# V projection of a cross attention as a 2x2 block product with seven block products, sums of blocks on POOL

## The reference

```python
x = x + _L0_xattn_ref(_layernorm(x), ctx_4096, Wq, Wk, Wv, Wo)
# in it, with H, KV, HD = 16, 4, 96 and G = H // KV
hidden = jnp.concatenate([context, latents], axis=1)      # (64, 289, 512)
q = (latents @ Wq.T).reshape(b, q_len, H, HD)
k = (hidden @ Wk.T).reshape(b, s_len, KV, HD)
v = (hidden @ Wv.T).reshape(b, s_len, KV, HD)             # (64, 289, 384)
# softmax(q k^T / sqrt(96)) v per head, then @ Wo.T
```

## Time and profile before

| | |
|---|---|
| three timed runs | 2138.29, 2140.99, 2141.76 us (median 2140.99) |
| the profiled execution | 2136.47 us, its span 2134.4 us |
| PE busy, over the span | 2059.4 us (96%) |
| DVE, ACT, POOL busy | 1308.7 us (61%), 683.7 us (32%), 248.3 us (12%) |
| mean granted TensorE clock | 0.989 |

### The profile page before, as it was taken

How to read it: one execution, slowest core, us unless ns; L and a number is a source line. 1 busy time by engine, 2 the same in 40 slices (tenths; PEclk the granted TensorE clock), 3 DMA queues, 4 the chain that set the end, 5 groups by cost and what they waited for, 6 DMA issues and landing times. The chain is left out here.

```text
span 2134.4 us, 33623 instructions
## 1 busy us (share of the span) xinstructions
PE 2059.4 (96%) x10660; PEld 1480.4 (69%) x10660; DVE 1308.7 (61%) x4451; ACT 683.7 (32%) x1861; POOL 248.3 (12%) x360
## 2 busy tenths in 40 slices
PE   7999999999999999999999999999899999779998
PEld 5778677777767778677777867777566666466665
DVE  3736547484654747456483755747577777677885
ACT  2333333333332433333242433333223223122222
POOL 0000000000000000000000000000233333133332
PEclk9999999999999999999999999999999999889999
DMA  7101000010000101001010000120100000000000
GB/s 289 31 15 31 23 24 30 24 30 24 24 20 24 30 24 30 24 24 30 14 37 16 30 23 24 30 86 1 45 1 1 1 0 29 0 1 21 21 15 25
DMA packets 51991, 62.14 MB, mean 29 GB/s; under 512 B 14193, under 2 KB 47665, under 8 KB 51042
## 3 DMA queue, kind: packets, MB, share of 16 engines
q1 hardware_dynamic: 51938, 61.46, 9.1%
HBM read 54.00 MB, written 4.29 MB: 27 GB/s over the span
## 5 line engine op out<-in xcount | busy, mean ns | idle before, releaser
L345 PE MATMUL psLane<-hid,WkT 128*128 128x289 f32 x1536 | 404.0, 408 | 0.0
L352 PE MATMUL psLane<-WvT,hid 128*128 128x384 f32 x1024 | 348.7, 486 | 0.0
L345 PEld LDWEIGHTS psLane<-hid,WkT 128*128 128x128 f32 x1536 | 284.1, 190 | 72.7
L352 PEld LDWEIGHTS psLane<-WvT,hid 128*128 128x128 f32 x1024 | 189.8, 190 | 109.7
L537 ACT ACTIVATE probs<-psLane,nmax 128x289 f32<-128x289 f32 x256 | 126.2, 498 | 423.6 <-DVE nmax L640 423.6
L505 ACT ACTIVATE KT<-psLane 96x289 f32<-96x289 f32 (+2 forms) x384 | 155.8, 406 | 153.3 <-PE psLane L345 151.0
L298 POOL TENSOR_TENSOR tails<-probs,unit 128x66 f32<-128x66 f32 x128 | 38.1, 297 | 1387.3 <-ACT probs L537 1387.3
L678 DVE MAX8 top<-work 128x8 f32<-128x257 f32 x512 | 180.3, 414 | 2.7
L335 PE MATMUL psLane<-xnT,WqT 128*128 128x128 f32 x1536 | 176.6, 275 | 0.0
L335 PEld LDWEIGHTS psLane<-xnT,WqT 128*128 128x128 f32 x1536 | 174.8, 192 | 0.3
L663 DVE TENSOR_TENSOR X<-X,psLane 128x512 f32 (+1 forms) x16 | 11.0, 689 | 261.6 <-PE psLane L417 261.6
(11 more groups left out here) (190 smaller groups left out, 3138.2 us busy)
## 6 DMA issues: line engine op xcount, KB each, us to landing
hid<-in_ctxT SPq DMA_DIRECT2D x64, 514.0 KB, 3.8
y<-X SPq DMA_DIRECT2D x16, 256.0 KB, 2.0
X<-in_x SPq DMA_DIRECT2D x1, 3840.0 KB, 14.9
WqT<-in_WqT SPq DMA_DIRECT2D x4, 768.0 KB, 11.4
WoT<-in_WoT SPq DMA_DIRECT2D x1, 3072.0 KB, 21.7
Vtail<-Vlat SPq DMA_DIRECT2D x128, 24.0 KB
w_qkv<-in_w_qkv SPq DMA_DIRECT2D x2, 1536.0 KB, 6.5
w_ffn<-in_w_ffn SPq DMA_DIRECT2D x2, 1024.0 KB, 8.0
```

Of the source, the lines that this page charges most:

```text
L345: mm = pe.matmul(out[:, 0:S], WkT[:, c, P * k:P * k + P], hid[:, j, c, :], start=(c == 0), stop=(c == DC - 1))
L352: mm = pe.matmul(out[:, 0:KW], hid[:, j, c, P * s:P * s + P], WvT[:, c, :], start=(c == 0), stop=(c == DC - 1))
```

## The change

The V projection of rows 0 to 255 of a batch, (256 x 512) by (512 x 384), is taken as a product of 2x2 blocks: rows by their half `s`, features by their half `k`, columns by their half `n` (VH = 192). Instead of eight block products there are seven (Winograd's form of Strassen's scheme), each of 2 matmuls of 128x192. Four sums of blocks of `hid` per batch (`vsums`) and, once, four sums of weight blocks (`vweights`) are made on POOL. The seven products go through PSUM in four fills (`V_FILLS`), ACT copies each fill into `vproducts`, and POOL adds them up into `V` in seven steps. `vweights`, `vproducts` and `vsums` lie in the space of `early["w_ffn"]` and `early["w_o"]`, weights of the next phase, so their loads are issued later (`square_in`), after the last batch's V.

```diff
+VH = KW // 2
+V_FILLS = ((1, 6), (7, 5), (3, 4), (2,))
...
+            def sum_rows(t, j):
+
+                b = TB * t + j
+                rows = lambda s, k: hid[:, j, 2 * k:2 * k + 2, P * s:P * s + P]
+                pool.wait_ge(ctx_in[j], 16 * (t + 1))
+                before = (t, 7 * j - 1) if j else (t - 1, 27)
+                if not (isinstance(t, int) and (t, j) == (0, 0)):
+                    pool.wait_ge(kv_filled, kv(*before) + 1)
+                pool.tensor_tensor(vsums[0], rows(1, 0), rows(1, 1), ALU.add).then_inc(vsum_step, 1)
+                pool.tensor_tensor(vsums[2], rows(0, 0), rows(1, 0), ALU.subtract).then_inc(vsum_step, 1)
+                pool.wait_ge(vsum_step, 4 * b + 2)
+                pool.tensor_tensor(vsums[1], vsums[0], rows(0, 0), ALU.subtract).then_inc(vsum_step, 1)
+                pool.wait_ge(vsum_step, 4 * b + 3)
+                pool.tensor_tensor(vsums[3], rows(0, 1), vsums[1], ALU.subtract).then_inc(vsum_step, 1)
...
+            def add_first(t, j):
+
+                b = TB * t + j
+                pool.wait_ge(kv_evac, kv(t, 7 * j + 3) + 1)
+                pool.tensor_tensor(u2, product(1), product(6), ALU.add).then_inc(vpost_step, 1)
+                pool.wait_ge(kv_evac, kv(t, 7 * j + 4) + 1)
+                pool.wait_ge(vpost_step, 3 * b + 1)
+                pool.tensor_tensor(u3, u2, product(7), ALU.add).then_inc(vpost_step, 1)
+                pool.wait_ge(vpost_step, 3 * b + 2)
+                pool.tensor_tensor(u4, u2, product(5), ALU.add).then_inc(vpost_step, 1)
+                wait(pool, av_done, 4 * b - 4)
+                pool.tensor_tensor(v_block(j, 1, 1), u3, product(5), ALU.add).then_inc(v_ready, 1)
+
+            def add_second(t, j):
+
+                b = TB * t + j
+                pool.wait_ge(kv_evac, kv(t, 7 * j + 5) + 1)
+                pool.wait_ge(vpost_step, 3 * b + 3)
+                pool.tensor_tensor(v_block(j, 0, 1), u4, product(3), ALU.add).then_inc(v_ready, 1)
+                pool.tensor_tensor(v_block(j, 1, 0), u3, product(4), ALU.subtract).then_inc(v_ready, 1)
+                pool.wait_ge(kv_evac, kv(t, 7 * j + 6) + 1)
+                pool.tensor_tensor(v_block(j, 0, 0), product(1), product(2), ALU.add).then_inc(v_ready, 1)
...
-            def v_part(t, j, s):
-                out = next_bank(t, 5 * j + 3 + s)
-                for c in range(DC):
-                    mm = pe.matmul(out[:, 0:KW], hid[:, j, c, P * s:P * s + P], WvT[:, c, :],
-                                   start=(c == 0), stop=(c == DC - 1))
...
+            def v_part(t, j, f):
+                out = next_bank(t, 7 * j + 3 + f)
+                for i, n in enumerate(V_FILLS[f]):
+                    if n == 6:
+                        pe.wait_ge(vsum_step, 4 * (TB * t + j) + 4)
+                        if isinstance(t, int) and (t, j) == (0, 0):
+                            pe.wait_ge(vweight_step, 4)
+                    mm = v_product(out[:, VH * i:VH * i + VH], j, n)
                 mm.then_inc(kv_filled, 1)
...
                 if g == 0:
-                    pe.wait_ge(kv_evac, kv(t, 5 * j + 4) + 1)
+                    pe.wait_ge(v_ready, 4 * b + 4)
...
-            def evac_v(t, j, s):
+            def evac_v(t, j, f):
+                act.wait_ge(kv_filled, kv(t, 7 * j + 3 + f) + 1)
+                if f == 0:
+                    wait(act, v_ready, 4 * (TB * t + j))
+                n = len(V_FILLS[f])
+                act.activation(vproducts[:, 2 * f:2 * f + n, :].rearrange("p a n -> p (a n)"),
+                               psKV[:, kv_bank(t, 7 * j + 3 + f), 0:VH * n], ACT.Copy).then_inc(kv_evac, 1)
...
+                    sp.wait_ge(kv_filled, kv(NT - 1, 27) + 1)
+                    sp.wait_ge(v_ready, 4 * B)
+                    for k, name in (("w_o", "w_o0"), ("w_ffn", "w_ffn0")):
+                        sp.dma_start(early[k][:], a[name]).then_inc(square_in, 16)
```

More of the change, by code:

```diff
@@ L112, in phase_a @@
         V = sb("V", [P, 2, 2, KW])
+        spare = [early[k][:].rearrange("p c n -> p (c n)") for k in ("w_ffn", "w_o")]
+        vweights = spare[0][:, 0:8 * VH].rearrange("p (i c n) -> p i c n", i=4, c=2)
+        vproducts = spare[1][:, 0:7 * VH].rearrange("p (i n) -> p i n", i=7)
+        vsums = [spare[i // 2][:, (8 - i // 2) * VH + 2 * P * (i % 2):][:, 0:2 * P].rearrange("p (c n) -> p c n", c=2)
+                 for i in range(4)]
         Vlat = sb("Vlat", [P, KW])
@@ L300, in body @@
             def body(t, first, last):
+                add_first(t, 0)
+                add_second(t, 0)
                 for j in range(TB):
[L302 to L305, removed]
+                    gather_tails(t, j, 0)
+                    if j < TB - 1:
+                        sum_rows(t, j + 1)
+                    else:
+                        add_second(t, j)
+                        if not last:
+                            sum_rows(t + 1, 0)
+                    if j == 1:
+                        next_rstd() if last else rstd_of(t + 1)
+                    gather_tails(t, j, 1)
+                    if j < TB - 1:
+                        add_first(t, j + 1)
+                    if j < TB - 2:
+                        add_second(t, j + 1)
@@ L347, in k_part, with v_product @@
                 mm.then_inc(kv_filled, 1)
[L349 to L353 removed]
+            def v_product(out, j, n):
+                rows = lambda s, k: lambda c: hid[:, j, 2 * k + c, P * s:P * s + P]
+                summed = lambda i: lambda c: vsums[i][:, c, :]
+                block = lambda k, n: lambda c: WvT[:, 2 * k + c, VH * n:VH * n + VH]
+                combined = lambda i: lambda c: vweights[:, i, c, :]
+                left, right = {1: (rows(0, 0), block(0, 0)), 2: (rows(0, 1), block(1, 0)), 3: (summed(3), block(1, 1)),
+                               4: (rows(1, 1), combined(3)), 5: (summed(0), combined(0)), 6: (summed(1), combined(1)),
+                               7: (summed(2), combined(2))}[n]
+                for c in range(2):
+                    mm = pe.matmul(out, left(c), right(c), start=(c == 0), stop=(c == 1))
+                return mm
+            def v_part(t, j, f):
[6 more added lines that the diff above has]
+                    mm = v_product(out[:, VH * i:VH * i + VH], j, n)
                 mm.then_inc(kv_filled, 1)
@@ L436, in body @@
                 k_part(t, 0, 2)
-                v_part(t, 0, 0)
-                v_part(t, 0, 1)
+                for f in range(4):
+                    v_part(t, 0, f)
                 if first:
@@ L555, in body @@
                     evac_k(t, 0, k)
-                evac_v(t, 0, 0)
-                evac_v(t, 0, 1)
+                for f in range(4):
+                    evac_v(t, 0, f)
                 if first:
@@ L584, in body @@
                         evac_v(t, j + 1, 0)
+                        evac_v(t, j + 1, 1)
                     else:
```

96 lines of the change are left out of this document (61 added, 35 removed).

## The result

The changed kernel takes 2099.07 us (median of 4 runs, 2098.84 to 2099.63); the kernel before, in the same set, 2139.64 us (4 runs, 2133.64 to 2141.76). The ratio is 0.982, with a 95% interval of 0.980 to 0.984. The forecast was 2110, the range 2103 to 2124: the direction was right, the gain larger than the range allowed. The medians differ by 40.6 us; profile against profile it is 2136.47 - 2099.63 = 36.8 us, where the prediction's sum had 29.5. Later sets put the median of the kernel before at 2135.23 to 2137.89, so 2 to 4 of the 40.6 us are the spread of its runs.

The account below looks back on a forecast made before the run. PE was taken as the bound, busy 92.19 of a tile's 92.30 us. A tile saves 3 x 0.55 + 0.27 = 1.92 us, 16 tiles 30.7, net 29.5; forecast 2110 us, range 2103 to 2124 for 8 in 10.

Parts of the forecast that it names:

- the pace of V: V's matmuls on PE: 165 ns per 192-column record, 28 records in 4.62 us instead of 5.17, 0.55 us saved per batch.
- the last batch of a tile: values starts 0.27 us sooner, held by POOL's adds; less 0.05, plus 0.05 at v_latents, 0.27 us gained per tile.
- start and end: First batch's wait for Vtail and lower clock behind it, 1 us charged; last tile's exponentials holding PE, 0.3 us less gained.
- sums hidden: POOL's 11 operations per batch, 6.8 us of some 16 us, delay nothing in batches 0 to 2 of a tile.
- The baseline: Profiled 2136.5 less 29.5 gives 2107; the timed median, 4.5 us higher, gives 2111.5; 2110 was taken.
- The lower bound of the pace: V's 192-column records on PE at cycles alone, 160 ns each: 0.69 us saved per batch, 44 us in all.
- The full gain: Rival: with adds of 0.5 us and a sooner OT copy the last batch saves 0.55 too; 35 us, 2105 us, 10%.
- no wait at product 6 or for a bank: PE finds POOL's sums ready at product 6, and ACT's copies free the two PSUM banks in time, 0.3 us to spare.
- The estimate that the prediction drew from the Trainium skill: V's matmuls at 87 ns for 192 columns against 114 for 384: slower by 0.6 us per batch; not used in the sum.
- DVE and POOL hold each other up: Rival: a hold of one add at mask, 0.57 us, loses 9 us, two such places 18; 2119 to 2128, 18%.
- The slower rival: POOL's three adds become the path at values of a tile's last batch; with three holds 22 us lost, 2163, 6%.

Follow-up runs that it names:

- Experiment 1: The kernel before with each V fill made as two halves of 192 columns, all eight block products, no sums: 2140.08 us, 1.0012.
- experiment 4: The first tile's Vtail loads issued ahead of those of X and WoT: in the changed kernel 2095.46 us, in the kernel before 2132.44 us.
- Experiment 2: The changed kernel without any of POOL's sums, PE's work the same, V not computed: 2099.77 us, 0.983.
- experiment 3: The changed kernel with more POOL adds ahead of the last three of every batch: one add 2108.63 us, four adds 2181.37 us.
- experiment 7: The changed kernel with one more DVE operation of 192 elements behind mask per batch: two SBUF inputs 2101.29 us, one input 2100.08 us.
- experiments 5 and 6: Changed kernel with values released before POOL's last add, 2106.29 us; changed kernel with DVE's OT copy ahead of MAX8 in a tile's last batch, 2108.18 us.

## Why the forecast was too cautious

Of the 10.9 us between 2110 and 2099.1, 7.3 us are in the sum and 3 in what it was set against; the rest is rounding and the spread of runs. The 7.3 are three terms: 2.9 for the pace of V, 3.2 for the last batch of a tile, 1.2 for start and end. The mechanism was right (PE is the bound, sums hidden, the last batch gains less); two of its terms were mis-sized, and none of them alone would have left the range.

- **The pace, mis-sized.** "On the line between the two it costs [...] 165 ns": measured 162.5. The line was drawn through the 128-column stream, which pays 5 ns over its cycles, while 192 columns pay 2.5 like 384. A batch saves 0.61 us, not 0.55, which for the 48 batches that the sum gave this term is 2.9 us. Experiment 1 found the same pace with no change to anything else.
- **The last batch, read at the wrong instruction.** The two starts were right within 0.12 us, but the gain was read off `values`, 0.27 us, with 0.05 given and 0.05 taken. The next in the queue, `v_latents`, starts when DVE's `hid` copy ends, before as after, and it is its start that the next tile inherits. That copy follows `xt` and not `values`. The prediction had 0.37 us for `xt`; carried on to `v_latents` by the 2.04 us between the two in the earlier trace rows it gives S+6.37 against S+6.74, 0.37 and not 0.27. Measured is 0.49 at both: the other 0.12 is `xt` itself, since the `OT` copy started at S+3.62 and took 0.54 us, where the prediction had S+3.7 and 0.56. Less 0.02 for the first half of V that is 0.47, 0.2 us more for each of 16 tiles, 3.2 us. With both terms a tile is 3 x 0.61 + 0.47 = 2.30 us instead of 1.92.
- **The start and the end, 1.2 us charged and none lost in sum.** The prediction charged 1 us for the start and 0.3 at the end (30.7 less these is 29.4, not 29.5). The waiting that it named is there: the first `values` starts 0.30 us sooner (50.35 against 50.65), where it is 0.78 without the wait (47.32 against 48.10, experiment 4). But the stretches at the two ends gain 3.21 + 1.84 = 5.05 us where nothing waits, 0.45 more than two tiles, and that makes up for it; the 0.3 at the end did not come, since 1.84 is three times 0.61. The prediction also took the clock as the same in both kernels. It fell behind the start's wait in the kernel before alone, and behind the last projection's wait in the changed one alone; that these two cancel is luck.
- **The baseline.** The sum gave 2107 from the profiled execution; I went up to 2110 for the median of the timed runs, 2141. Later sets of the kernel before have medians of 2136.11 (15 runs), 2135.23 (9) and 2137.89 (17): the profiled time of 2136.5 was near the middle, and three runs were few to move a forecast on. 3 us.
- **The range.** The lower bound of the pace, 160 ns, gave 44 us of gain in the prediction's own words, and the measured pace lies halfway to it; a range that ended at 2103 left that out. "The full gain" (2105) was one of the rivals, given 10%; it gave the last batch its whole 0.55 but kept the pace at 165, and even it was 6 us short.
- **What held.** PE stayed the bound, 28 records per batch, no wait at product 6 or for a bank, POOL's operations of 0.59 us for 192 elements and 0.64 to 0.73 for 256 against 0.57 and 0.71, all hidden in batches 0 to 2, DVE's order, full clock in the tiles. Experiment 2 confirms that the sums are free, experiment 3 that the next 0.59 us on POOL would not be. The estimate that the prediction drew from the Trainium skill ("TensorE: Matmul & The Clock Gate", Back-to-back issue gap), a loss of 0.6 us per batch, fell with the rows, as weighed; on the straight line between the two values given there, 192 columns are 89 ns and not 87, so it should have read 0.7.
- **The rivals.** "DVE and POOL hold each other up" came true in part and decided nothing: `mask` takes 0.23 us in the median as before (0.28 at most), the norm 0.60 instead of 0.54, and `top_last`, which the prediction did not name, up to 0.45 instead of 0.18 (experiment 7), all away from the path. The slower rival had its place right, `values` of the last batch, and was priced too low: it counted the wait and no clock, where experiment 3 found that 2.58 us of wait cost 5.57.

## What to carry to other kernels

Here, with PE the bound and POOL idle, a 2x2 block product with seven products paid an eighth of the product's time, less 2.5 ns for each further record (0.61 of 5.16 us), and 435 us of sums cost nothing. Book the gain of a pipeline's last step where the next stage starts, one instruction behind the one that you watch; and before adding a wait or moving a copy, look at what stands behind it on its engine (experiments 5 and 6 each cost 0.3 to 0.4 us per tile for 0.1 hoped for). The cheapest gain was outside the change: a small transfer that is needed first, issued ahead of two large ones (experiment 4). And compare looped stretches before medians: two executions that differ in the clock behind one wait differ by 1.4 to 3 us.

## What the runs showed of the hardware

**A held POOL operation can last as long as a chain of DVE's.** In the one-off start of the changed kernel, all engines in order of time:

```profile
28.40 6.42 DVE L827 SCALAR_TENSOR_TENSOR band<-work,taps,band 128x384 f32<-128x384 f32 x12
28.49 6.79 POOL L356 TENSOR_TENSOR w_o<-w_o 128x192 f32<-128x192 f32 x1 [0.71 <-ACT w_o L619]
```

An add of 0.59 us lasted 6.79 us, to 0.46 us past the end of twelve DVE operations with two SBUF inputs. It cost nothing: the last add of that V ends at 38.1 us and its first `values` starts at 50.35. The Trainium skill ("SBUF — State Buffer", Who interferes with whom) names such DVE instructions as the ones that exclude POOL; this trace and experiment 7 agree (761 and 787 ns at most with two inputs, 347 and 594 with one).

**The clock falls behind short waits, too, but not behind all of one length.** Each trace has the same wait of 1.45 us before the last projection. In seven of the twelve the granted clock stayed at 1.00; in five (the changed kernel, experiments 1, 5 and both of 7) it was 0.50 to 0.64 over the 4 us behind, and the projection took 1.4 to 3.1 us longer. Behind the start's wait for `Vtail` it stayed at 1.00 in four traces (1.29 to 1.65 us) and was 0.50 to 0.64 in six (1.87 to 3.12 us). With four more adds a wait of 2.28 us left it at 1.00, and waits of 2.57 us cost 3.0 us of clock in tile after tile. So longer waits go with the lower clock, but the length alone does not decide, and what else does stays open.

**The fixed part of a float32 record** at full clock is 2.5 ns at 192 and 384 columns, and 5 ns at 128.
